# Image pair 0 of a dynamic convolution: x in five transfers, an earlier sum of exponentials, a range added up in PSUM, fewer constant products

## What is computed

```python
h = gn(x)                                    # 32 groups of 2 channels
a = relu(mean_hw(h) @ fc1_w.T + fc1_b)
att = softmax(a @ fc2_w.T + fc2_b)           # (32, 4)
agg_w = einsum('bk,koihw->boihw', att, weight)
out = x + conv3x3(h, agg_w) + (att @ bias)[:, :, None, None]
```

## Time and profile before

| | |
|---|---|
| median of 3 runs | 305.23 us (304.73 to 305.49) |
| the profiled execution | 304.7 us |
| its span | 302.9 us |
| mean granted TensorE clock | 0.998 |
| TensorE products busy | 297.3 us (98%) |
| VectorE, ScalarE, GpSimd busy | 246.0, 189.8, 17.7 us |
| first real product starts | 14.26 us |

### The profile page before, as it was taken

One profiled execution on the slowest core, in us unless ns is written; L12 is line 12 of the kernel. 1 busy time (PEld: TensorE's weight loads), 2 busy tenths in 40 slices (PEclk: granted clock), 3 DMA queues, 4 the chain that ended last, 5 costly groups with the idle time before them and its releaser, 6 DMA issues.

```text
span 302.9 us, 15877 instructions
## 1 busy us (share of the span) xinstructions
PE 297.3 (98%) x7066; PEld 273.2 (90%) x7066; DVE 246.0 (81%) x799; ACT 189.8 (63%) x246; POOL 17.7 (6%) x30
## 2 busy tenths in 40 slices
PE   8899999999999999999999999999999999999995
PEld 6678997799978997799999999999999999999874
DVE  3898998989999999998998989699696978956000
ACT  3766739194683927385496869567685866768222
POOL 2221040402100000000000000000000000000000
PEclk9999999999999999999999999999999999999999
DMA  7957875737547575846808898685758342332333
GB/s 266 307 166 191 284 231 161 218 131 197 161 150 224 161 208 173 225 157 170 239 26 236 243 232 276 155 257 164 209 135 235 96 122 70 111 101 80 95 112 104
DMA packets 26868, 53.62 MB, mean 177 GB/s; under 512 B 6064, under 2 KB 16432, under 8 KB 26800
## 3 DMA queue, kind: packets, MB, share of 16 engines
q1 hardware_dynamic: 26576, 52.53, 58.6%
q10 hardware_dynamic: 224, 0.07, 0.1%
HBM read 26.89 MB, written 25.69 MB: 174 GB/s over the span
## 4 chain that ended last, share of the span: by engine, by line
PE 95%; DMA 2%; DVE 1%; SPq 0%; issue 0%; POOL 0%; ACT 0%; DVEq 0%
PE acc L1063 94%; DMA x<-x 2%; SPq L315 0%; DVE stats L443 0%; PE tiny L1004 0%; PE acc L1031 0%; PE acc L1043 0%; POOL rstd L414 0%; DVE mv L478 0%; DVE o L791 0%; ACT wh L863 0%; PE tiny L1016 0%; DVE mix L642 0%; PE tiny L1010 0%; DVE sums L490 0%
## 5 line engine op out<-in xcount | busy, mean ns | idle before, releaser
L1063 PE MATMUL acc<-xh,wh 64*64 64x385 f16 (+5 forms) x2304 | 112.6, 325 | 0.3 <-ACT wh L863 0.3
L1063 PE MATMUL acc<-xh,wl 64*64 64x385 f16 (+5 forms) x2304 | 112.4, 325 | 0.0
L1063 PE MATMUL acc<-xl,wh 64*64 64x385 f16 (+5 forms) x2304 | 111.7, 325 | 0.0
L1063 PEld LDWEIGHTS acc<-xl,wh 64*64 64x64 f16 x2304 | 91.4, 107 | 5.9
L1063 PEld LDWEIGHTS acc<-xh,wl 64*64 64x64 f16 x2304 | 90.6, 107 | 6.7
L1063 PEld LDWEIGHTS acc<-xh,wh 64*64 64x64 f16 x2304 | 89.6, 107 | 7.4 <-ACT wh L863 0.5
L913 ACT ACTIVATE o<-acc,par 128x392 f32<-128x392 f32 (+1 forms) x64 | 43.0, 672 | 56.8 <-PE acc L1063 56.8
L457 DVE BATCH_NORM_STATS2 stats<-x 128x6 f32<-128x448 f32 x105 | 61.2, 618 | 1.9
L834 ACT ACTIVATE xh<-x,xof,xsc 128x1568 f16<-128x1568 f32 x24 | 40.5, 1692 | 25.2 <-DVE xof L544 24.7
L701 DVE TENSOR_TENSOR xl<-x,xh 128x1568 f16<-128x1568 f32 x28 | 49.8, 1783 | 3.4 <-ACT x L801 3.2
L592 DVE SCALAR_TENSOR_TENSOR mix<-w_sb,ex,mix 128x576 f32<-128x576 f32 (+1 forms) x69 | 42.9, 621 | 0.5
(11 more groups left out here) (106 smaller groups left out, 161.8 us busy)
## 6 DMA issues: line engine op xcount, KB each, us to landing
x<-x SPq DMA_DIRECT2D x60, 392.0 KB, 4.1
out<-o SPq DMA_DIRECT2D x36, 196.0 KB, 3.8
out<-o SPq DMA_DIRECT2D x72, 98.0 KB, 2.8
out<-o SPq DMA_DIRECT2D x8, 588.0 KB, 3.7
out<-o SPq DMA_DIRECT2D x16, 294.0 KB, 4.3
x<-x SPq DMA_DIRECT2D x3, 448.0 KB, 4.5
w_sb<-w_t SPq DMA_DIRECT2D x2, 576.0 KB, 3.9
out<-o SPq DMA_DIRECT2D x7, 112.0 KB, 2.2
```

Source lines behind the costliest of these rows:

```text
L1063: ins = nc.tensor.matmul(pixels[:, top:bottom, left:right], weights[i][halves[m], tap * C:(tap + 1) * C], window, start=start and step == ...
```

## The change

Pair 0 of x comes in five transfers in place of four: the last two chunks come apart. `exsum` is computed ahead of the diagonals. `first_range` multiplies the deviations first and then `wnorms` into the same column, and the product for `weights_bound` is moved behind `part_sum`, into `tiny[0]`, with a semaphore of its own. `keep_warm` 1, 2 and 3 go from 8, 12 and 6 products to 4, 6 and 2.

```diff
-PIECES = ((0, 2), (2, 4), (4, 5), (5, 7))
-PIECE_OF = (0, 0, 1, 1, 2, 3, 3)
+PIECES = ((0, 2), (2, 4), (4, 5), (5, 6), (6, 7))
+PIECE_OF = (0, 0, 1, 1, 2, 3, 4)
...
-WARM_PRODUCTS = (38, 8, 12, 6, 3, 3)
+WARM_PRODUCTS = (38, 4, 6, 2, 3, 3)
...
                     nc.vector.reciprocal(rsum[:], exsum[:]).then_inc(dch, 1)
-                    dve.wait_ge(s_range, 3)
+                    dve.wait_ge(s_range, 1)
...
                 dve.wait_ge(s_const, 3)
+                nc.vector.tensor_reduce(exsum[:], ex[:], AX.X, ALU.add).then_inc(s_exsum, 1)
 
                 for k in range(SUMMED_SHARES):
                     nc.vector.tensor_scalar(diagonals[:, k, :], eye[:], ex[:, k:k + 1], None, ALU.mult).then_inc(s_diagonal, 1)
-                nc.vector.tensor_reduce(exsum[:], ex[:], AX.X, ALU.add).then_inc(s_exsum, 1)
...
-                dve.wait_ge(s_range, 3)
-                nc.vector.tensor_scalar(wbound[:], tiny[1][:, WEIGHTS:WEIGHTS + 1], 1.0 / C, None,
+                dve.wait_ge(s_weights_range, 1)
+                nc.vector.tensor_scalar(wbound[:], tiny[0][:, WEIGHTS:WEIGHTS + 1], 1.0 / C, None,
...
-                pe.wait_ge(s_wnorms, 1)
-                nc.tensor.matmul(tiny[1][:, WEIGHTS:WEIGHTS + 1], scale[:], wnorms[:],
-                                 start=True, stop=True).then_inc(s_range, 1)
-                nc.tensor.matmul(tiny[1][:, RANGE:RANGE + 1], scale[:], wnorms[:], start=True, stop=False)
+
                 pe.wait_ge(s_first_std, 1)
                 for m in range(2):
                     nc.tensor.matmul(tiny[1][halves[m], RANGE:RANGE + 1], ones[halves[m], 0:C], std[0][halves[m], :],
-                                     start=False, stop=True).then_inc(s_range, 1)
+                                     start=True, stop=False)
+                pe.wait_ge(s_wnorms, 1)
+                nc.tensor.matmul(tiny[1][:, RANGE:RANGE + 1], scale[:], wnorms[:], start=False, stop=True).then_inc(s_range, 1)
+
+            def weights_range():
+
+                nc.tensor.matmul(tiny[0][:, WEIGHTS:WEIGHTS + 1], scale[:], wnorms[:],
+                                 start=True, stop=True).then_inc(s_weights_range, 1)
...
             part_sum()
+            weights_range()
             keep_warm(4)
```

More of the change, by code:

```diff
@@ L215, in dynamic_conv @@
         s_exsum = sem("s_exsum")
+        s_weights_range = sem("s_weights_range")
         s_eye_exsum = sem("s_eye_exsum")
```

## The result

The changed kernel took 306.42 us in the median of 20 runs (304.32 to 307.73), against 305.03 of the kernel before beside it (304.73 to 306.0, 20 runs): a ratio of 1.0037, 95% interval 1.0023 to 1.0052. It is slower, by 0.4%. The forecast was 304.6, its range ended at 306.2, and the case of a falling clock, which it gave 28%, is what happened in most runs.

The account below looks back on a forecast made before the run. TensorE, busy 98% of the span, was taken as the bound, leaving only the time before the first real product. 0.49 from transfers plus 0.12 from the third stretch gave 0.61: 305.23 - 0.61 = 304.6 us, range 304.0 to 306.2.

Parts of the forecast that it names:

- the case of a falling clock: Rival, 28%: TensorE runs at 1.2 GHz from about 11.6 on, giving 306.1 (305.7 to 306.4).
- Bound of the kernel, effect of the first real product: TensorE busy 98% of the span; every tenth the first real product (14.26) moves should move the end a tenth.
- Five transfers: Start of pair 0: splitting x's last piece removes VectorE's idle before the last statistics; gain 0.49 (0.19 to 0.49).
- They don't move by more than 0.08: ScalarE's squares start at 8.79, first weights land at 8.71; so squares move at most 0.08 and `wnorms` hardly.
- `exsum` first and the residual: `eye_exsum` ends at 11.95, out of the way; residual goes at 12.27, 0.66 after the part sum (0.59 to 0.66).
- The start of the part sum: TensorE starts the part sum at 11.61, after two diagonals at 11.55 and a hand-over of 0.06.
- The moved product: Range product behind the part sum takes 0.24 (0.2 to 0.38); TensorE's queue ends at 13.64, first real product 13.65.
- both cost nothing and their removal gives nothing: Four constant products after x's last piece and six after the statistics stand in waits; removing them changes nothing.
- What they cover is the clock: Constant products keep TensorE's clock at 2.4 GHz; they take 421 ns at the start, later 272.
- 2.5 us of light work: At the span's tail, products end at 299.5 and granted clock is 0.50 at 302.00, so it can fall that fast.
- Its price: 1.5, bounds 1.1 to 1.8: Cost of the clock's fall: 1.5; 1.1 if back halfway through the constants, 1.8 if some real products run low.

Follow-up runs that it names:

- all products: Changed kernel with the constant products of the kernel before (38, 8, 12, 6, 3, 3); 304.36 us, ratio 0.9975; run again 304.83 us, ratio 0.9996.
- after, place 3 back: Changed kernel with only `keep_warm` 3 back at six products, against the kernel before; 305.28 us, ratio 1.0004, falls in 6 of 12 runs.
- after, place 2 back: Changed kernel with only `keep_warm` 2 back at twelve products, against the kernel before; 305.78 us, ratio 0.9998, falls in 7 of 12 runs.
- before, few products: Kernel before with only the change's constant products (38, 4, 6, 2, 3, 3); 306.10 us, ratio 1.0026, falls in 10 of 12 runs.
- all products, range as before: Changed kernel with the old constant products and `first_range` in its old order, against the kernel before; 305.44 us, ratio 1.0015.
- all products, weights later: Changed kernel with the old constant products, first weights issued when piece 1 has landed instead of piece 0; 306.89 us, ratio 1.0059.
- after, places 2 and 3 back: Changed kernel with `keep_warm` 2 and 3 back at twelve and six, `keep_warm` 1 left at four; 305.00 us, ratio 1.0009.
- before, five transfers: Kernel before with only x's five transfers added; 305.06 us, ratio 1.0000, falls in 0 of 12 runs.

## Why the prediction was wrong

- **Bound of the kernel, effect of the first real product: right.** 0.43 earlier there and 0.4 less span, with all products.
- **Five transfers: right in direction, 0.34 for 0.49.** The statistics run without idle, but at 0.588 each, and piece 0 landed 0.07 later. What the term left out is that it passes on only as the range's new order lets it: alone it is worth nothing (305.06). In the prediction the two stood as separate terms; they are one.
- **"They don't move by more than 0.08": wrong in most executions.** The prediction took the first weights' landing from one profile with four transfers, 4.2 us, and gave ScalarE 0.08 of slack on it. With five it is 4.8 to 5.1 in eight of eleven profiles, and then the root of the weights' bound sets the range: of the profiles with the split and the new order and without a fall, four with late weights were at 304.77 to 305.17, the one with weights on time at 304.38. Nothing in the profile of before showed it. The Trainium skill (page "DMA: Bandwidth & Descriptors", section "Bandwidth") asks for transfers of at least 1 MiB, which speaks against this edit, and the prediction set it aside because landings went by bytes. In the changed kernel the last piece of x paid nothing beyond the scatter (landed by 7.5, with four transfers 7.3 to 7.6); the transfer behind them did.
- **`exsum` first and the residual: right.** With all products the residual's load follows the part sum by 0.52, the prediction's lower bound (0.53), not by the 0.66 taken. The start of the part sum was 0.22 later than forecast, 0.15 of it from the sums.
- **The moved product: right.** TensorE's queue and the scaled weights come together: six products from 12.98, 0.82 long, and the real ones at 13.83.
- **"both cost nothing and their removal gives nothing": this is the step that failed.** The prediction wrote next to it "What they cover is the clock", so it had the mechanism, but its sum puts the removal of ten products at nothing and that of the four of place 3 at a gain, and the fall of the clock is left to a rival at 28%. The fall came in 15 of 20 runs. Taking the products away costs 306.42 - 304.36 = 2.06 us in the changed kernel and 306.10 - 305.03 = 1.07 in the old one, where 10 of 12 runs fell. The rows at hand spoke for it less clearly than the prediction says: what it calls "2.5 us of light work" in the tail is 2.4 us without any product, from 299.6 to 302.0 (the row below). The Trainium skill (page "TensorE: Matmul & The Clock Gate", section "HAM oscillation — how this bites in real kernels") names long gaps without a matmul as the cause, and that was given weight against the fall. The longest gap between products in the profile after is 1.07 us, ahead of L1011, and the clock fell: the measurement decides, and short gaps that add up do it too.

```profile
299.60:302.00 2.40, 0.00 (x0) 0.00 (x0) 0.51 (x1) 0.48 (x1) 0.00 (x0) 0.95 0.72 191
```

- **Its price: 1.5, bounds 1.1 to 1.8, was right for one kind of fall** (306.14 - 304.60 = 1.54) and too low for the other, more frequent kind (307.41 - 304.60 = 2.81). The low stretch says why: at half speed 3.41 us lose at most 1.7, and 6.83 at most 3.4. The upper bound had only the constants, the part sum and some real products low; in the profile after, 36 real products ran at 531 ns and half pace, the last of them starting at 18.0. So even the rival's own 306.1 lay below the median.
- **What the removal does besides.** In three profiles with all products the twenty of places 1 and 2 held the sums on TensorE back by 0.4 to 0.7 us, so "cost nothing" is not always so either.
- **Spread.** The prediction priced a fall as one yes or no for the median. The result is a mixture, whose median sits in the middle group.

What stays open: why a fifth transfer of x delays the weights behind it, why the low stretch is sometimes twice as long, and that only in the changed kernel with fewer products, and what makes a few runs without a fall slow (305.98 to 306.58 in four sets).

## What to carry to other kernels

Work that only keeps TensorE going is not free to remove because it stands in a wait: count how busy TensorE is over the whole light stretch and not only the length of its gaps, and see the granted clock in each of a dozen runs, since one profile may show none of it (the kernel before fell in 5 of 123 runs, and not in its profile). When one stage is sped up, look for the other input that ends just behind it: here the weights had 0.08 us of slack, and it is gone when a transfer lands half a microsecond late. Terms that end in the same wait are not added; each is worth what the others let through.

## What the runs showed of the hardware

- TensorE's clock fell to 0.50 with no gap of products over 1.1 us in four of six profiles (the first four rows); in the other two the longest gap was 1.14 and 1.49. Not every run of these kernels fell, and the busy time in this one stretch doesn't settle it: 2.14 fell and 2.01 did not. Before, few products, was even busy for 1.43 of the 1.70 us from 11.5 to 13.2 before its clock fell. What the profiles show (in the second row the last 0.6 us of the stretch are already at the low clock):

| profile | TensorE busy from 8.5 to 11.5, us | clock at 0.50 |
|---|---|---|
| after | 1.65 | 11.62 to 18.45 |
| after, place 3 back | 1.71 | 10.88 to 14.29 |
| after, place 2 back | 1.72 | 12.46 to 15.88 |
| before, few products | 1.81 | 13.34 to 16.76 |
| all products, range as before | 1.81 | 12.60 to 16.01 |
| all products, weights later | 2.14 | 13.26 to 16.67 |
| after, places 2 and 3 back | 2.01 | stays at 1.00 |
| before | 2.55 | stays at 1.00 |
| all products | 2.58 | stays at 1.00 |

- The fall comes in two sizes, mean clock 0.992 to 0.994 with 3.41 us at 0.50 (1.54 us lost) and 0.987 to 0.988 with 6.83 us (2.81 lost), though TensorE was busy without a gap from 13.2 on in the latter.
- At the start the constant products went from 421 to 272 ns between 4.2 us (place 3 back) and 7.2 us (before, five transfers), with the same 38 products issued from 1.35 on. The trace has no granted clock under 1.00 there, so this is read from the durations.
- Constant products of 256 columns take 421 ns at the low level and 272 at the high, real ones of 385 and 392 columns 531 and 327.
- A transfer issued behind five transfers of x lands after 4.3 or after 4.8 to 5.1 us, behind four after 4.2 to 4.5, with the same bytes of x.
